# TensorE makes du*B for six states a step in the first halves of batches 1 to 3, with a third product bank

## The reference

```
x  = in_proj(ctx);  u = silu(conv4(x));  dt, B, C = x_proj(u);  delta = softplus(dt_proj(dt))
state[n] = state[n] * exp(delta * A[n]) + (delta * u) * B[n]        # n = 0..15, over time
y = sum_n state[n] * C[n];   x1 = x + (y + D * u) * silu(layernorm(x))
z = layernorm(x1);  route: softmax of a (1024*1024 -> 8) product, top 2 experts
out = x1 + (z + experts(z)) @ w3.T + b3
```

## Time and profile before

| | before |
|---|---|
| median of 3 runs | 2447.03 us (2446.58 to 2447.78) |
| profiled execution | 2449.12 us |
| its span, first to last instruction | 2447.1 us |
| mean granted TensorE clock | 0.904 |
| busy share: PE, DVE, ACT, POOL | 81%, 87%, 65%, 62% |

### The profile page before, as it was taken

The page is one execution under the profiler, slowest core; times in us unless marked ns, Lnnn a source line. Parts: engine busy times, 40 slices in busy tenths (PEclk is TensorE's granted clock), DMA queues, the critical chain, the costliest instruction groups (busy, mean ns, idle before and its releaser), DMA issues.

```text
span 2447.1 us, 32499 instructions
## 1 busy us (share of the span) xinstructions
PE 1991.9 (81%) x10584; PEld 1180.8 (48%) x10584; DVE 2121.5 (87%) x2694; ACT 1601.4 (65%) x2357; POOL 1525.9 (62%) x1061
## 2 busy tenths in 40 slices
PE   6898889986857987996757897898785787787899
PEld 2677667754533553443434454354453354344344
DVE  5899799979998999989999899998999899899311
ACT  2687877766668868655658977855666857854500
POOL 0698677767755765666766675576775577577111
PEclk9899999997878999997878998899786899899899
DMA  5311515555512944566621554466461174467512
GB/s 176 126 40 58 194 53 172 185 196 200 196 52 70 318 146 130 164 208 206 235 84 69 201 201 141 149 223 207 166 221 31 52 254 164 141 213 284 205 57 72
DMA packets 199290, 383.00 MB, mean 157 GB/s; under 512 B 30513, under 2 KB 96049, under 8 KB 199122
## 3 DMA queue, kind: packets, MB, share of 16 engines
q1 hardware_dynamic: 195952, 380.46, 46.2%
q10 hardware_dynamic: 3170, 0.47, 0.1%
HBM read 346.79 MB, written 34.08 MB: 156 GB/s over the span
## 4 chain that ended last, share of the span: by engine, by line
PE 32%; DVE 22%; issue 22%; ACT 16%; POOL 6%; DMA 1%; DVEq 1%; POOLq 0%; ACTq 0%; SPq 0%
DVE h L1547 10%; PE dense L1161 10%; PE dense L989 5%; POOL h L876 5%; ACT dA L1270 4%; DVE dense L1523 4%; PE dense L927 3%; ACT L1239 3%; PE dense L1086 2%; DVE u L1383 2%; PE dense L975 2%; PE dense L939 2%; PE dense L1144 2%; PE dense L996 2%; ACT hs L1357 2%
## 5 line engine op out<-in xcount | busy, mean ns | idle before, releaser
L876 POOL TENSOR_TENSOR h<-h,Cb 128x1024 f32<-128x1024 f32 x512 | 1208.3, 2361 | 375.0 <-DVE h L1547 349.1
L1270 ACT ACTIVATE dA<-delta,Av 128x512 f32<-128x512 f32 x1024 | 703.3, 716 | 390.9 <-DVE h L1547 387.9
L989 PE MATMUL dense<-ident,h 128*128 128x128 f32 x4096 | 601.6, 298 | 155.0 <-POOL h L876 154.3
L989 PEld LDWEIGHTS dense<-ident,h 128*128 128x128 f32 x4096 | 518.1, 155 | 309.7 <-POOL h L876 222.3
L1547 DVE TENSOR_TENSOR_SCAN h<-dA,state,dense 128x512 f32<-128x512 f32 x512 | 628.8, 1268 | 18.5 <-PE dense L989 7.6
L1547 DVE TENSOR_TENSOR_SCAN h<-dA,dense 128x512 f32<-128x512 f32 x512 | 597.2, 1205 | 12.9 <-PE dense L989 8.4
L1523 DVE TENSOR_TENSOR dense<-dense,Bb 128x512 f32<-128x512 f32 x864 | 552.4, 687 | 1.6
L1161 PE MATMUL dense<-w3h,xT 128*128 128x512 f32 x832 | 384.8, 598 | 1.3 <-DVE xT L1503 1.3
L870 POOL COPY state<-h 128x2 f32<-128x2 f32 x256 | 47.7, 186 | 319.3 <-DVE h L1547 317.6
L927 PE MATMUL dense<-ctxs,win 128*128 128x512 f32 x432 | 209.8, 631 | 10.2 <-ACT szT L1299 9.0
L1161 PEld LDWEIGHTS dense<-w3h,xT 128*128 128x128 f32 x832 | 148.3, 192 | 137.7 <-issue 135.8
(11 more groups left out here) (167 smaller groups left out, 2009.9 us busy)
## 6 DMA issues: line engine op xcount, KB each, us to landing
sww<-in_sw SPq DMA_DIRECT2D x167, 512.0 KB, 4.3
Cb<-bc_scratch SPq DMA_DIRECT2D x64, 512.0 KB, 6.6
Bb<-bc_scratch SPq DMA_DIRECT2D x54, 512.0 KB, 4.8
w3h<-in_sw SPq DMA_DIRECT2D x52, 512.0 KB, 8.0
w3h<-in_w3T SPq DMA_DIRECT2D x52, 512.0 KB, 5.2
row<-x_scratch SPq DMA_DIRECT2D x40, 512.0 KB, 4.8
xz<-in_x SPq DMA_DIRECT2D x64, 256.0 KB, 4.7
xt<-in_x SPq DMA_DIRECT2D x64, 256.0 KB, 4.1
```

What stands on the lines that cost most here:

```text
L876: e.tensor_tensor(h[:, s:s + 2, :], h[:, s:s + 2, :], Cb[:, 2 * q:2 * q + 2, :], ALU.mult).then_inc(prod_done, 1)
L989: mm = e.matmul(yT[:, k, :], h[:, 2 * ((PAIRS * g + q) % RH) + i, k * P:(k + 1) * P], ident[:], is_transpose=True, start=False, stop=(q == ...
L1270: e.activation(dA[:, i % RA, :], delta[:, st % 2, :], ACT.Exp, scale=Av[:, j * N + n:j * N + n + 1]).then_inc(dA_done, 1)
```

## The change

In the first half of batches 1 to 3 (24 steps, `pe_step`), the six states of pairs 2, 4 and 6 (`HALF_PAIRS`) have their du*B made by TensorE. These steps have three product banks, F1, M0 and M1, handed out in turn by a table (`ProductBanks`); the turned du takes a place in that order too, also in batch 0, where it had bank F0. duT has one buffer instead of two, and ScalarE copies it in slot 7 of the step before, right behind copy_du, instead of in slot 0. In batches 1 to 3 TensorE meets `first_sum` where it did, behind the slot's second product.

Diagonals are made by GpSimd for all chunks but the first: the broadcast B is loaded, and an affine_select in place keeps its diagonal. These are ten in the second half of batch 0 (VectorE's ten multiplies there go) and six in each of the three first halves of batches 1 to 3, placed two to six slots behind the load.

Since F1 is now taken in those steps, the experts' work of `u` = 0 does without it: turns use F0 alone, at other slots; hidden uses F0 and F2, the latter also the bank of expert_out, so that the second hidden matmul of a pair waits for out_add of the pair before; tiles alternate between F0 and F2. For `u` = 1 the turns use F1 in place of F2. b3 is loaded in halves of 512 columns, once for each of the four groups of tiles in a batch.

The diff, cut:

```diff
 PE_PAIRS = (1, 2, 4, 5, 6)
+HALF_PAIRS = (2, 4, 6)
...
+def pe_step(g):
...
 def on_pe(g, n):
-    return g < STEPS and n // 2 in PE_PAIRS
-def product_bank(g, n):
-    return (F1, M0, M1)[(N * g + n) % 3] if g < STEPS else (M0, M1)[n % 2]
+    return pe_step(g) and n // 2 in (PE_PAIRS if g < STEPS else HALF_PAIRS)
+class ProductBanks:
+    def __init__(self):
+        self.bank, self.before = {}, {}
+        order, held = [F1, M0, M1], {}
+        for g in range(ALL):
+            for n in range(N):
+                if n == N - 2 and g + 1 < ALL and pe_step(g + 1):
+                    self.place(order, held, ("turn", g + 1), order)
+                self.place(order, held, ("product", g, n), order if pe_step(g) else [k for k in order if k != F1])
+    def place(self, order, held, name, among):
+        k = among[0]
+        self.bank[name], self.before[name] = k, held.get(k)
+        held[k] = name
+        order.remove(k)
+        order.append(k)
+BANKS = ProductBanks()
 class Schedule:
     def forward(self, b, rows):
         self.logits(b, rows, [TB + k for k in range(TB)], [5, 6, 15, 20], [8, 13, 18, 23], [4] * TB, RING_A)
         for k in range(TB):
-            self.add(b, 14 + 5 * k, "turn", 0, k, 0)
-            self.add(b, 14 + 5 * k, "turn", 0, k, 1)
...
-        if b == 1:
-            self.add(b, 33, "b3_load")
+            for i in (0, 1):
+                t = ((11, 13), (17, 19), (24, 26), (27, 29))[k][i]
+                self.add(b, t, "turn", 0, k, i)
+                self.add(b, t + 1, "turned", 0, k, i)
...
+                self.add(b, at[W3C * (TB * dh - 1)] + 3 if dh else at[0] - 2, "b3_load", u, dh)
...
-            return [((what, *args), F0 + i if u == 0 or b == NB else F2)]
+            return [((what, *args), F0 + i if b == NB else F1 if u else F0)]
...
-            return [((what, *args, i), first + i) for i in (0, 1)]
+            second = F2 if b < NB and args[0] == 0 else first + 1
+            return [((what, *args, i), (first, second)[i]) for i in (0, 1)]
...
-            return [((what, *args[:3]), F0 + (TB * args[1] + args[2]) % 2)]
+            m = TB * args[1] + args[2]
+            if b == NB:
+                return [((what, *args[:3]), F0 + m % 2)]
+            return [((what, *args[:3]), (F1, F0)[m % 2] if args[0] else (F0, F2)[m % 2])]
...
-        duT = sb("duT", [P, 2, TB, P])
+        duT = sb("duT", [P, TB, P])
+        b3half = sb("b3half", [P, QD])
...
+        def diag_index(c, n):
...
+            elif before:
+                e.wait_ge(duT_done, 1 + turns_of_du(before[1]) + 1)
         def bc_value(c, q):
-            return 1 + sum(16 if on_pe(J * i, 2 * q) else 32 for i in range(c + 1))
+            return 1 + 32 * (c + 1) - (16 if on_pe(0, 2 * q) else 0)
+        def b3_of(b, uu, dh):
...
-                for i, dst in ((N, Cb),) if on_pe(J * c, 2 * q) else ((0, Bb), (N, Cb)):
+                for i, dst in ((N, Cb),) if c == 0 and on_pe(0, 2 * q) else ((0, Bb), (N, Cb)):
...
+                        if b < NB or dh == 0:
+                            e.wait_ge(b3_added, 1 + n)
+                        else:
+                            e.wait_ge(duB_pe_done, 1 + pe_index(ALL, 0))
+                        e.dma_start(dst, b3[dh * QD:(dh + 1) * QD].partition_broadcast(P)).then_inc(b3_loaded, 16)
...
+            def diagonal_b(c, n):
+                e.wait_ge(bc_loaded[n // 2], bc_value(c, n // 2))
+                e.affine_select(out=Bb[:, n, :].rearrange("p (k t) -> p k t", k=TB), in_=Bb[:, n, :].rearrange("p (k t) -> p k t", k=TB),
+                                compare_op=ALU.is_equal, fill=0.0, base=0, pattern=[[0, TB], [-1, P]], channel_multiplier=1) \
+                    .then_inc(diag_done, 1)
...
+                    for n in range(N):
+                        at = n // 2 + 4 + n % 2
+                        if j == J - 1 and at == q and c + 1 < NB * TH and on_pe(g + 1, n):
+                            diagonal_b(c + 1, n)
+                        if j == 0 and at == SLOTS + q and c and on_pe(g, n):
+                            diagonal_b(c, n)
...
-            def turn_du(g):
+            def turn_du(g, bank):
                 e.wait_ge(du_s_done, 1 + g + 1)
-                e.wait_ge(duT_done, 1 + g)
                 for k in range(TB):
-                    mm = e.transpose(dense[:, F0, k * P:(k + 1) * P], du_s[:, k * P:(k + 1) * P], ident[:])
+                    mm = e.transpose(dense[:, bank, k * P:(k + 1) * P], du_s[:, k * P:(k + 1) * P], ident[:])
                 mm.then_inc(du_turned, 1)
...
-                    e.wait_ge(h_done, 1 + bank_free(g, n))
+                    e.wait_ge(diag_done, 1 + diag_index(g // J, n) + 1)
+                wait_product_bank(e, ("product", g, n))
                 for k in range(TB):
-                    mm = e.matmul(dense[:, product_bank(g, n), k * P:(k + 1) * P], duT[:, g % 2, k, :],
+                    mm = e.matmul(dense[:, BANKS.bank[("product", g, n)], k * P:(k + 1) * P], duT[:, k, :],
                                   Bb[:, n, k * P:(k + 1) * P], start=True, stop=True)
                 mm.then_inc(duB_pe_done, 1)
             def times_b_at(i):
                 g, n = divmod(i, N)
-                if on_pe(g, n):
+                if g < ALL and on_pe(g, n):
                     times_b(g, n)
...
                 st, q = divmod(t, SLOTS)
                 g, c = STEPS * b + st, TH * b + st // J
                 th, j = divmod(st, J)
-                if b == 0:
-                    if q == 1 and j == J - 1 and g + 1 < STEPS:
-                        turn_b(c + 1, count(b, "x_proj", th) + 1)
-                    if q == 2:
-                        first_sum(g)
+                if b == 0 and q == 2:
+                    first_sum(g)
+                if b < NB:
                     times_b_at(N * g + 2 * q + 3)
-                    if q == SLOTS - 2 and g + 1 < STEPS:
-                        turn_du(g + 1)
+                    if q == SLOTS - 2 and g + 1 < ALL and pe_step(g + 1):
+                        if not pe_step(g):
+                            last = ("tile", 1, NQ - 1, TB - 2)
+                            e.wait_ge(evac[bank_of(b, *last)], 1 + count(b, *last) + 1)
+                        wait_product_bank(e, ("turn", g + 1))
+                        turn_du(g + 1, BANKS.bank[("turn", g + 1)])
                 for what, *a in PLAN.slots[b][t]:
                     name = (what, *a)
...
+                            e.wait_ge(h_done, 1 + N * (STEPS * b + J))
                         for n in range(J // 2):
                             d = (J // 2) * i + n
                             mm = e.transpose(dense[:, bank, n * P:(n + 1) * P], rows[:, d * P:(d + 1) * P], ident[:])
...
                     first_sum(g)
                 if b < NB and q >= 2:
                     sum_pair(g, q - 1)
-                if b == 0 and q == SLOTS - 1:
+                if b < NB and q == SLOTS - 1:
                     times_b_at(N * g + 2 * q + 4)
                 for what, *a in PLAN.slots[b][t]:
...
                 e.copy(du[:], du_s[:]).then_inc(du_done, 1)
...
-                    e.wait_ge(duB_pe_done, 1 + pe_index(g - 1, 0))
-                e.copy(duT[:, g % 2].rearrange("p k e -> p (k e)"), dense[:, F0, :]).then_inc(duT_done, 1)
+            def copy_duT(g, bank):
+                e.wait_ge(du_turned, 1 + turns_of_du(g) + 1)
+                e.copy(duT[:].rearrange("p k e -> p (k e)"), dense[:, bank, :]).then_inc(duT_done, 1)
             def exp_ln_table():
...
                                      scale=Av[:, j * N + n:j * N + n + 1]).then_inc(dA_done, 1)
                     if q == 0:
-                        if g and g < STEPS:
...
                             .then_inc(zn_done, 1)
                     if q == SLOTS - 1 and g + 1 < ALL:
                         copy_du(g + 1)
+                        if pe_step(g + 1):
...
             def diagonal_b(c, n):
                 e.wait_ge(b_turned, 1 + c + 1)
-                if c:
```

More of the change, by code:

```diff
@@ L222, in tail @@
         for dh in range(NQ):
+            self.add(b, 46, "b3_load", 0, dh)
+        for dh in range(NQ):
             for u in (0, 1):
@@ L370, in build @@
         tail_rows = [Bb[:, 2 * k:2 * k + 2, :].rearrange("p n t -> p (n t)") for k in range(TB)]
-        b3row = duT[:].rearrange("p a k t -> p a (k t)")
         hs_tail = sww[:, 1].rearrange("p e d -> p (e d)").rearrange("p (i t) -> p i t", i=2)
@@ L500, in chunk_block, with turns_of_du, wait_product_bank @@
             return G // STEPS, G // J % TH, G % J
+        made = [0]
+        for g_ in range(ALL):
+            made.append(made[-1] + sum(on_pe(g_, m) for m in range(N)))
         def pe_index(g, n):
-            return 2 * len(PE_PAIRS) * min(g, STEPS) + sum(on_pe(g, m) for m in range(n))
+            return made[g] + (sum(on_pe(g, m) for m in range(n)) if g < ALL else 0)
         def vec_index(g, n):
             return N * g + n - pe_index(g, n)
-        def bank_free(g, n):
```

(39 more changed lines are left out.)

24 lines of the change are left out of this document (7 added, 17 removed).

## The result

The changed kernel takes 2455.27 us (median of 6 runs, 2451.3 to 2458.36) where the kernel before takes 2447.28 beside it. The ratio is 1.0032, 95% interval 1.0019 to 1.0045: slower by 0.3%, about 8 us, where 14 us less were forecast. The profiled execution took 2453.99 us, its span is 2452.3, and the mean granted clock went from 0.904 to 0.935.

A forecast was written before the change was run, and what follows sets the result against it. VectorE was taken to bound plain steps, the expert loop steps 5 and 6, TensorE steps 8 and 15, with step 7 nearly full on both. Terms -16.5 - 6 + 12 - 5 + 2 = -13.5 us gave 2433, range 2405 to 2456.

The forecast's parts named there:

- its two prices: From slot 2's last scan to slot 3's first: 2.9 us at full clock (stand 1.6), 5.4 at low clock (stand 4.2).
- the term for steps 0 to 4: Plain steps, batches 1 to 3: each worth -2.2 to +0.4 us, taken as -1.1; -16.5 in all, ends -33 and +6.
- VectorE's saving: Three pairs of products leave VectorE in each first-half step of batches 1 to 3: 3.8 us a step.
- a slot and more of slack: Behind slot 3's first scan in plain steps, later sums were claimed to have this much room.
- Steps 5 and 6: Steps with hidden and gelu, batches 1 to 3: -2 us a batch, -6 in all, ends -15 and +6.
- Step 7: Step with tiles, TensorE-bound: +5 us in batches 1 and 2, +2 in batch 3; +12 together, ends +6 and +18.
- Batch 0's -5: Ten diagonal multiplies, 6.4 us as pairs, leave VectorE in step 7 of batch 0: -5 us, ends -8 and 0.
- the milder form of B: Half of B's total slowdown: 2458 us in the sum; the range's upper end was given as 2456.
- B: Slot 3: product 8 ahead of first_sum makes the sum late and eats the saving: +22 us, 2469; chance 0.17.
- C: Steps don't get shorter, waiting elsewhere for as much; only batch 0 gains: -3 us, 2444; chance 0.12.
- A: Added products keep TensorE at 2.4 GHz, slot 3's stand 1.6 us throughout: -38 us, 2409; chance 0.23.

The follow-up runs named there:

- The repeated product: Changed kernel with state 5's product in batches 1 to 3 issued four times over, same matmuls into the same bank: 2448.11 us, ratio 0.9995 to the kernel before.
- the moved `first_sum`: Changed kernel with first_sum ahead of state 8's product in slot 2, batches 1 to 3: 2403.18 us, ratio 0.9818 to the kernel before.
- the late sum: Kernel before with first_sum and pair 0's sum put behind state 8's product in slot 2 of batch 0: 2483.78 us, ratio 1.0144.

## Why the prediction was wrong

The prediction had the bound right, and the mechanism too. It found the wait, its place (slot 3's first scan, for the sum of pair 0), its makers (state 8's product ahead of `first_sum`) and its two prices; in steps 0 to 4 of batch 1 five of VectorE's nine waits for PE, with 16.4 of 18.0 us, stand at slot 3's first scan (2.98, 3.04, 2.94, 3.70 and 3.70 us). **The step that failed is the size of the term for steps 0 to 4:** "I take -1.1, half way", fifteen times, -16.5 in all, came out at +6.2. That is 22.7 us, more than the spans' whole miss of 18.7 (+5.2 for -13.5); the other terms together came out 4 us better than forecast. (The medians miss by 22 because the profiled execution of the changed kernel is 1.3 us below its median, where that of the kernel before was taken as 2.1 above.) Three things make up the 22.7 (less 1.4 us of waits that these steps had before):

- *The low clock.* The prediction argued that two new products ahead of slot 2 would lift the clock in some places. In the 15 plain steps the stretch from the end of slot 2's scans to the next scan was 4.0 to 4.9 us, as against 2.7 at full clock (forecast 2.9 and 5.4). VectorE stood 50.4 us there in all, 3.4 a step, not the 2.7 implied: 10 us. Of these 3 are a slip: half way between -2.2 and +0.4 is -0.9, not -1.1. The repeated product shows that the rest was the clock: the stand became 1.5. Both prices were somewhat high, since product, transposes and sum overlap by about 0.2 us each (product and transposes start at 579.18 and 581.02, 1.84 us apart, the product taking 2.05); all at 1.2 GHz the stretch was 4.9, not 5.4, and the stand 3.7. Against the 3.8 counted as saved, even that would not have made a step longer. It took the next two items as well.
- *VectorE's saving.* 3.8 us a step was read off the groups' busy time. The instructions overlap their neighbours by some 0.1 us, so a pair that goes takes less than its 1.27 us from the engine's line: over steps 0 to 4 of batch 1 busy time fell by 3.49, 3.40, 3.58, 3.25 and 2.55, a mean of 3.25 (in step 4 one small routing instruction, L1654, took 1.90 us in place of 1.08). That is 0.55 less than the 3.8, and 8 us over 15 steps.
- *Small waits behind it.* The prediction gave the sums "a slot and more of slack" past slot 3. They had less: waits of 0.2 to 0.7 us at slot 0 of the next step and at slot 6 add up to some 6 us.

The other terms. Steps 5 and 6 gained 8.4 us where 6 were forecast, and the clock went to 1.00 in batch 1, as it was said it might; but that they agree is partly luck. 6.0 of the 8.4 are batch 1's, whose two steps together were 3 us longer than those of batches 2 and 3 before, and in the run without the diagonals of batch 0 steps 5 and 6 of batch 2 took 40.0 and 42.1 us, not 38.1 and 40.4, with nothing changed in them. Step 7 took 36.7, 36.7 and 35.7 us where 38, 38 and 35.3 were forecast: the idle time was right (1.1 us), TensorE's busy time was 35.5 and not 37.0. Batch 0's -5 was an assumption about the path; the run without the multiplies gives 0. GpSimd's select of 128x512 had been put at 0.6 us and no row; it now has one, and is hidden:

```profile
L912 POOL TENSOR_SCALAR_AFFINE_SELECT Bb<-Bb x28: 624/634/652, 286.5 to 1727.7; 128x512 f32<-128x512 f32 x28
```

No wait of TensorE for a duT copy (there was one of 2.2 us before), for a diagonal made by GpSimd or for b3 shows up; two of VectorE, 3.0 us in all, in step 7 of batch 0 and at its end have no releaser in the profile and stay unexplained. Leaving the products out puts the price of all that at 0, but for the diagonals of batches 1 to 3. The granted clock of the first halves was 0.92 and 0.90 in batches 1 and 3, as forecast (about 0.9): the mean rose, the one place did not. The measured 2455 lies just inside the stated range, whose upper end, "the milder form of B, 2456", should by the prediction's own sum be 2458.

The rivals. B came true: its mechanism is the one that the moved `first_sum` shows, and its +6 for steps 0 to 4 is the +6.2 measured. Its total of +22 was too high mainly since steps 5 and 6 gained 8.4 us where it had +5. That the +6 fits is partly luck: B asked for a sum later than 5.1 us, which no step has; with the saving at 3.25 the point lies at 4.4 (1.2 covered), which eight of the 15 plain steps pass (4.8 to 4.9 us; the other seven have 4.0 to 4.4). C had the steps not getting shorter, but by several waits that add up; it was one place for 16.4 of 18.0 us in batch 1. A, the clock that comes up, is wrong for the changed kernel's plain steps (its stand of 1.6 us is what the repeated product brought); once the order is right the clock is 0.953 over the kernel and step 0 takes 28.7 us. The pages of the Trainium skill that stood beside A and B can be judged by that: "TensorE: Matmul & The Clock Gate" (What's actually happening) has the clock follow activity, and the trace agrees, but more work in a step (26.0 us instead of 22.4) brought 0.90 over the step and still 1.2 GHz in the one place that counted, after 1.74 us of standing. Nearer is what the same page of the Trainium skill says in "A second HAM failure mode: psum-queue depth-cycling": short pauses between groups of matmuls can make the clock swing and cost throughput. The trace agrees as far as the pauses go: with the late sum step 2 of batch 0 itself fell from 1.00 to 0.88. It does not show which pauses do it: in steps 5 and 6 of the changed kernel's three batches TensorE stood the same 1.21 us ahead of state 8's product each time, and that ran at 2.4 GHz four times and at 1.2 twice.

## What to carry to other kernels

When work moves to an engine with room, look first at what it stands in front of in that engine's in-order queue. An instruction that must wait for another engine makes everything behind it wait as well; put the items that others wait for ahead of it. Here two lines of order were worth 52 us, six times the change's own effect and with the other sign.

When a wait's price has two values by the clock and the verdict changes between them, the middle is not a forecast. A step's mean clock does not tell the clock of one place: in 12 of the 15 plain steps the product ran at 1.2 GHz, in steps whose mean was up to 0.95. Cheaper than to guess is to change the order so that the price is not paid at either clock.

A saving read off busy times is too large where instructions overlap: three pairs of 1.27 us gave 3.25 to 3.6 us a step, and 2.55 in one.

## What the runs showed of the hardware

A kernel can be made faster by useless work of TensorE: 72 repeated products took some 7 us off it, through the clock (the stand before slot 3 was 1.5 us in place of 2.8 to 3.7). And the reverse: an order that makes TensorE stand 1.7 us for a scan lengthened steps 1 to 6 of batch 0 by 3.0 to 3.8 us each where 1.5 had been worked out at full clock, since in most of them the four transposes and the product that follow the pause ran at 1.2 GHz (1.06 and 2.05 us, against 0.60 to 0.66 and 1.13). A pause as long did not bring it everywhere: in step 9 of that batch the product ran at 2.4 GHz after 1.83 us. What decides is not shown. GpSimd's affine_select of 128x512 fp32 in place takes 0.63 us, half of its two-input multiply of the same size (1.27).
